# A fused convolution and quadratic-patch kernel in float32: matmul rounds regrouped by form, weight preparation spread over three engines, border taps on eight tiles

## What is computed

```python
y3 = conv(gn(x), w3, 'SAME') + b3          # 3x3, 32 -> 32 channels
y5 = conv(gn(x), w5, 'SAME') + b5          # 5x5, 32 -> 32 channels
stacked = [y5] + [y3 shifted by (ey, ex), zero padded, for the 9 shifts]
x = x + sum_g wr[c, g] * stacked[g] + br
spot = [1] + 3x3 patch of gn(x)            # 10 values a pixel and channel
x = x + einsum(spot[i] * spot[j], filters[o, c, i, j])
```

## Time and profile before

| | us |
|---|---|
| median of 3 runs (lowest, highest) | 365.67 (365.66, 366.77) |
| profiled execution | 365.12 |
| its span | 363.4 |
| first matmul starts | 30.07 |
| last matmul ends | 353.7 |
| PE busy | 323.6 |
| DVE, ACT, POOL busy | 188.3, 80.9, 5.2 |

### The profile page before, as it was taken

The page is one execution under the profiler, slowest core; times in us unless marked ns, Lnnn a source line. Parts: engine busy times, 40 slices in busy tenths (PEclk is TensorE's granted clock), DMA queues, the critical chain, the costliest instruction groups (busy, mean ns, idle before and its releaser), DMA issues.

```text
span 363.4 us, 15504 instructions
## 1 busy us (share of the span) xinstructions
PE 323.6 (89%) x7496; PEld 139.7 (38%) x7496; DVE 188.3 (52%) x227; ACT 80.9 (22%) x127; POOL 5.2 (1%) x28
## 2 busy tenths in 40 slices
PE   0006999999999999999999999999999999999990
PEld 0002544444544343344332247433334332247430
DVE  0399935504996035404499655429103679654036
ACT  1201025207337034500000003286000000000085
POOL 5000000000000000000000000000000000000000
PEclk9999999999999999999999999999999999999997
DMA  7943000000000000000000000055000000000046
GB/s 145 347 123 91 4 4 2 4 4 2 4 5 2 4 2 5 2 4 4 2 4 2 4 4 4 4 117 119 2 4 4 2 4 2 4 4 4 4 101 132
DMA packets 3297, 11.57 MB, mean 32 GB/s; under 512 B 804, under 2 KB 932, under 8 KB 3108
## 3 DMA queue, kind: packets, MB, share of 16 engines
q1 hardware_dynamic: 2656, 9.91, 10.1%
q10 hardware_dynamic: 484, 0.68, 0.8%
q0 software_dynamic: 96, 0.01, 0.5%
HBM read 6.40 MB, written 4.19 MB: 29 GB/s over the span
## 4 chain that ended last, share of the span: by engine, by line
PE 89%; DVE 5%; DMA 3%; ACT 1%; ACTq 1%; issue 0%; DVEq 0%
PE acc L570 87%; DMA w_in<-in_L_conv_w 3%; DVE raw L494 1%; PE acc L620 1%; DVE stats L449 1%; DVE folded L361 1%; PE acc L597 1%; ACT plane L265 0%; ACT folded L319 0%; ACTq L254 0%; ACTq L251 0%; DVE weight L362 0%; DVEq L81 0%; ACT w_taps L316 0%; PE acc L604 0%
## 5 line engine op out<-in xcount | busy, mean ns | idle before, releaser
L570 PE MATMUL acc<-product,weight 32*32 32x512 f32 (+1 forms) x4416 | 185.8, 601 | 0.0
L523 DVE TENSOR_TENSOR product<-plane 128x4096 f32<-128x4096 f32 x24 | 105.2, 4424 | 71.0 <-PE acc L570 70.9
L570 PE MATMUL acc<-plane,weight 32*64 32x512 f32 (+1 forms) x2048 | 102.0, 605 | 30.1 <-ACT plane L265 30.1
L570 PEld LDWEIGHTS acc<-product,weight 32*32 32x32 f32 (+1 forms) x4416 | 78.6, 111 | 106.8 <-issue 93.7
L570 PEld LDWEIGHTS acc<-plane,weight 32*64 32x64 f32 (+1 forms) x2048 | 39.5, 122 | 87.5 <-issue 84.7
L292 ACT ACTIVATE raw<-acc,offset_by_strip 32x512 f32<-32x512 f32 x44 | 29.8, 678 | 105.3 <-PE acc L570 104.6
L290 ACT ACTIVATE raw<-acc 32x512 f32<-32x512 f32 x48 | 28.2, 587 | 50.2 <-PE acc L570 49.5
L570 PE MATMUL acc<-plane,middle 32*64 32x512 f32 (+1 forms) x640 | 37.3, 593 | 0.0
L492 DVE COPY raw<-acc 32x512 f32<-32x512 f32 x16 | 11.1, 694 | 42.0 <-PE acc L570 41.7
L494 DVE TENSOR_SCALAR raw<-acc,offset_by_strip 32x512 f32<-32x512 f32 x20 | 15.1, 755 | 31.2 <-PE acc L570 30.8
L313 ACT ACTIVATE product<-plane 128x4096 f32<-128x4096 f32 x2 | 7.3, 3630 | 66.8 <-PE acc L570 66.7
(11 more groups left out here) (66 smaller groups left out, 45.1 us busy)
## 6 DMA issues: line engine op xcount, KB each, us to landing
raw<-in_x SPq DMA_DIRECT2D x8, 512.0 KB, 9.6
out<-raw SPq DMA_DIRECT2D x14, 256.0 KB, 3.0
filters_in<-in_L_conv_filters SPq DMA_DIRECT2D x4, 400.0 KB, 3.8
out<-raw ACTq DMA_DIRECT2D x2, 256.0 KB, 3.0
w_in<-in_L_conv_w SPq DMA_DIRECT2D x4, 100.0 KB, 3.3
w_in<-in_L_conv_w ACTq DMA_DIRECT2D x4, 36.0 KB
b_in<-in_L_conv_b POOLq DMA_DIRECT2D x2, 0.5 KB, 5.2
wr_in<-in_L_conv_wr ACTq DMA_DIRECT2D x1, 5.0 KB
```

Of the source, the lines that this page charges most:

```text
L523: nc.vector.tensor_tensor(product_rows(n), inner(g, 0, H), shifted(g, PRODUCTS[k]), ALU.mult)\
L570: return nc.tensor.matmul(acc[32 * s:32 * (s + strips), h, r, :], weights[32 * r:32 * r + 32, t:t + strips, :] .rearrange("p t c -> p (t c ...
```

## The change

- PE, stage 0: band 0 is now pairs of all five columns, borders, singles; band 1 is singles, borders, pairs, so that the next group's pairs follow in one round. `taps0`, `borders0` and `corners` replace the loop.
- PE, stage 1: `linear` and product 0 of both bands share three rounds; each later product does one form for both bands, and begins with the form the last one ended in. `PRODUCTS` is in another order for this, and the last two products are free only at `half_done`.
- Border columns: the right column goes to tiles (32r, 32(r+1 mod 4)), the left stays on (32r, 32r), and row taps and column taps alternate. ACT copies the right one with four instructions.
- Start: SP and ACT issue wr, w3 and w5 ahead of all images, ACT takes two of group 0's pieces, and SP takes the biases from POOL, behind group 0. DVE reorders w3 and goes on to the statistics. ACT scales the 3x3 taps once for each shift into `scaled3` (nine activations), POOL adds them to `folded` (nine adds, each waiting for the one before), and DVE transposes in two parts behind its part of the plane; PE waits for the first part for its first column.

```diff
-PRODUCTS = ((0, 0), (2, 2), (0, 1), (2, -2), (0, 2), (1, 2), (1, 1), (1, -2), (1, -1), (2, 1), (2, -1), (2, 0), (1, 0))
+PRODUCTS = ((0, 0), (0, 1), (2, 2), (2, -2), (1, 1), (1, -1), (2, 1), (1, 2), (0, 2), (2, -1), (1, -2), (1, 0), (2, 0))
...
-            if k == N_PRODUCTS - 1:
+            if k >= N_PRODUCTS - 2:
                 eng.wait_ge(half_done, N_HALVES + BANDS * (g + 1))
             else:
-                eng.wait_ge(product_used, (N_PRODUCTS - 1) * g + k + 1)
+                eng.wait_ge(product_used, (N_PRODUCTS - 2) * g + k + 1)
...
+        def load_small(eng, quarters):
+            if 0 in quarters:
+                eng.dma_start(wr_in[:, :], wr.rearrange("o g y x -> o (g y x)").partition_broadcast(GROUP))\
+                   .then_inc(small_in, 16)
+            else:
+                for r in range(GROUP):
+                    eng.dma_start(w5_in[32 * r:32 * r + 32, :], w5.rearrange("o c y x -> o (c y x)"))\
+                       .then_inc(taps5_in, 16)
+            for r in quarters:
+                eng.dma_start(w3_in[32 * r:32 * r + 32, :], w3.rearrange("o c y x -> o (c y x)")).then_inc(small_in, 16)
...
+            load_small(sp, (0, 1))
+            load_raw(sp, 0, (0, 2))
+            for n, v in enumerate((b3, b5, br)):
+                sp.dma_start(b_in[:, n:n + 1], v.rearrange("(o n) -> o n", n=1).partition_broadcast(GROUP))\
+                  .then_inc(bias_in, 16)
+            load_raw(sp, 1, range(PIECES))
...
+            pool.wait_ge(taps5_ready, 1)
+            five = folded[:, 0:TAPS0, :].rearrange("p (x y) c -> p x (y c)", x=5)
+            for n, (ey, ex) in enumerate(EY_EX):
+                pool.wait_ge(shift_scaled, n + 1)
+                three = scaled3[:, n, :, :].rearrange("p (x y) c -> p x (y c)", x=3)
+                part = five[:, ex + 1:ex + 4, C * (ey + 1):C * (ey + 4)]
+                nc.gpsimd.tensor_tensor(part, part, three, ALU.add).then_inc(shift_folded, 1)
+                if n < len(EY_EX) - 1:
+                    pool.wait_ge(shift_folded, n + 1)
...
+            load_small(act, (2, 3))
+            load_raw(act, 0, (1, 3))
...
+                nc.scalar.activation(columns[:, g, 0, :], acc[:, 1, 0, 0:H], ACT.Identity, bias=ring_bias[:, 14:15])
+                for r in range(GROUP):
+                    s = (r + 1) % STRIPS
+                    last = nc.scalar.activation(columns[32 * r:32 * r + 32, g, 1, :], acc[32 * s:32 * s + 32, 1, 1, 0:H],
+                                                ACT.Identity, bias=ring_bias[32 * s:32 * s + 32, 15:16])
...
-            nc.scalar.activation(w3_taps[:, :, :].rearrange("p (x y) c -> p x y c", x=3),
-                                 w3_in[:, :].rearrange("p (c y x) -> p x y c", y=3, x=3), ACT.Copy)
...
+            act.wait_ge(taps3_ready, 1)
+            for n, (ey, ex) in enumerate(EY_EX):
+                s = shift_index(ey, ex)
+                nc.scalar.activation(scaled3[:, n, :, :], w3_taps[:, :, :], ACT.Copy, scale=wr_in[:, s:s + 1])\
+                  .then_inc(shift_scaled, 1)
...
-            def fold_taps():
-                dve.wait_ge(taps_ready, 1)
...
-                    step(nc.vector.scalar_tensor_tensor(part, three, wr_in[:, s:s + 1], part, ALU.mult, ALU.add))
-                nc.vector.transpose(weight0[:, 0:TAPS0, :].rearrange("p t c -> p (t c)"),
-                                    folded[:, 0:TAPS0, :].rearrange("p t c -> p (t c)")).then_inc(weight0_ready, 1)
-                dve.wait_ge(weight0_ready, 1)
+            def reorder_taps():
+                dve.wait_ge(small_in, 80)
+                nc.vector.tensor_copy(w3_taps[:, :, :].rearrange("p (x y) c -> p x y c", x=3),
+                                      w3_in[:, :].rearrange("p (c y x) -> p x y c", y=3, x=3)).then_inc(taps3_ready, 1)
+            def turn_taps():
+                dve.wait_ge(shift_folded, len(EY_EX))
+                for a, b in ((0, 5), (5, TAPS0)):
+                    last = nc.vector.transpose(weight0[:, a:b, :].rearrange("p t c -> p (t c)"),
+                                               folded[:, a:b, :].rearrange("p t c -> p (t c)"))
+                    last.then_inc(weight0_ready, 1)
+                dve.wait_ge(weight0_ready, 2)
...
+                if phase == 0:
+                    turn_taps()
...
-            fold_taps()
+            reorder_taps()
...
-            def border_columns(g):
-                if g == 1:
+            def border_column_tap(g, t):
+                for side, col in enumerate((0, W - 1)):
+                    for r in range(GROUP):
+                        s = (r + side) % STRIPS
+                        at = PLANE_AT + t * PITCH + col
+                        last = nc.tensor.matmul(acc[32 * s:32 * s + 32, 1, side, 0:H],
+                                                weight0[32 * r:32 * r + 32, EDGE_AT + 5 * (2 + side) + t + 2, :],
+                                                plane[g][32 * r:32 * r + 32, at:at + (H - 1) * PITCH + 1:PITCH],
+                                                start=t == -2, stop=t == 2, tile_position=(32 * r, 32 * s))
+                return last
+            def borders0(g, h):
+                pe.wait_ge(edge_ready, 1)
+                if h == 0 and g > 0:
+                    wait_evicted(BANDS * g - 1)
+                for t in range(-2, 3):
+                    border_row_tap(g, h, t)
+                    if h == 0:
+                        last = border_column_tap(g, t)
+                if h == 0 and g == 1:
                     pe.wait_ge(weight1_ready, 1)
                     for s in range(STRIPS):
-                        nc.tensor.matmul(acc[32 * s:32 * s + 32, 1, 2, 0:2], weight1[0:32, CONST_AT, :],
-                                         ones[0:32, :], start=True, stop=True, tile_position=(0, 32 * s))
-                for t in range(-2, 3):
-                    for side, col in enumerate((0, W - 1)):
-                        for r in range(GROUP):
-                            at = PLANE_AT + t * PITCH + col
-                            last = nc.tensor.matmul(acc[32 * r:32 * r + 32, 1, side, 0:H],
-                                                    weight0[32 * r:32 * r + 32, EDGE_AT + 5 * (2 + side) + t + 2, :],
-                                                    plane[g][32 * r:32 * r + 32, at:at + (H - 1) * PITCH + 1:PITCH],
-                                                    start=t == -2, stop=t == 2, tile_position=(32 * r, 32 * r))
-                last.then_inc(columns_done, 1)
+                        last = nc.tensor.matmul(acc[32 * s:32 * s + 32, 1, 2, 0:2], weight1[0:32, CONST_AT, :],
+                                                ones[0:32, :], start=True, stop=True, tile_position=(0, 32 * s))
+                if h == 0:
+                    last.then_inc(columns_done, 1)
+                corners(g, h)
...
-            pe.wait_ge(weight0_ready, 1)
+            def taps0(g, h, pairs, start, stop):
+                for n, dx in enumerate(COLUMNS0):
+                    if g == 0 and h == 0 and pairs:
+                        pe.wait_ge(weight0_ready, min(n + 1, 2))
+                    if dx == 0:
+                        pe.wait_ge(middle_ready, g + 1)
+                    five = middle0[g] if dx == 0 else weight0[:, 5 * (dx + 2):5 * (dx + 3), :]
+                    last = column(h, plane[g], PLANE_AT, dx, range(-2, 3), five, start and n == 0,
+                                  stop and n == len(COLUMNS0) - 1, pairs)
+                return last
             for g in range(NG):
                 pe.wait_ge(plane_dve, g + 1)
                 pe.wait_ge(plane_act, g + 1)
-                for h in range(BANDS):
-                    if g > 0:
-                        wait_evicted(BANDS * (g - 1) + h)
-                    if h == 1:
-                        pe.wait_ge(columns_copied, g + 1)
-                    for pairs in (True, False):
-                        for n, dx in enumerate(COLUMNS0):
-                            if dx == 0:
-                                pe.wait_ge(middle_ready, g + 1)
-                            five = middle0[g] if dx == 0 else weight0[:, 5 * (dx + 2):5 * (dx + 3), :]
-                            if n == 2 and pairs:
-                                pe.wait_ge(edge_ready, 1)
-                                border_row(g, h)
-                                if h == 0:
-                                    if g > 0:
-                                        wait_evicted(BANDS * g - 1)
-                                    border_columns(g)
-                            last = column(h, plane[g], PLANE_AT, dx, range(-2, 3), five, n == 0,
-                                          n == len(COLUMNS0) - 1, pairs)
-                    last.then_inc(half_done, 1)
-            def taps1(g, h, k):
-                if k is None:
-                    for pairs in (True, False):
-                        for n, ix in enumerate((-1, 1, 0)):
```

(56 more changed lines are left out.)

72 lines of the change are left out of this document (30 added, 42 removed).

## The result

| | before | after |
|---|---|---|
| median (lowest, highest), us | 366.05 (365.66, 366.77) | 344.94 (344.8, 345.88) |
| ratio, 95% interval | | 0.9427 [0.9402, 0.9451] |
| span of the profiled execution | 363.4 | 343.1 |
| first matmul starts | 30.07 | 20.86 |

What follows compares the result with a forecast made beforehand. PE was taken to bound the kernel, busy 323.6 of 363.4 us. Start 19.5 + stream (323.66 - 9.3 - 2.4) + tail 9.7 = span 341.2; plus 1.7 and 0.55 gave 343.4, stated as 343.5; range 340.5 to 349, own range 340.5 to 345.

Steps and rivals of the forecast that it cites:

- Start 19.5: First matmul on PE expected at 19.5 instead of 30.07, a gain of 10.6 us; bounds 17 and 27.8.
- The plane's path: Before the first matmul: last image piece at 14.4, two statistics, then 3.9 us; ends at 19.5, last by a little.
- the weights' path: Before the first matmul: weights land at 8.0, ACT scales, POOL does nine adds, then a transpose; ends at 18.5.
- the rival: At the start: slow adds or late w3 make the weights set PE's start, 23 to 28; 347 to 352 us, chance 0.15.
- An add of 0.85: Each of POOL's nine adds at the start takes 0.85 us, DVE's 0.53 times 1.6.
- Rounds 9.3: PE's stream: fewer changes between pairs and singles, 84 rounds down to 25, save 9.3 us, range 8 to 10.
- Borders 2.4: Stage 0 border stretches: border columns on eight tiles instead of four save 2.4 us in all; 0.3 at the other end.
- The fullest-tile count (1.98): Border stretch on eight tiles: the fullest tile has a row's 0.70 and a column's 1.28, so 1.98 us instead of 3.26.
- column tiles that do not run together: Stage 0 borders: reading strided columns may be limited by the row group; 2.1 us comes back, 345.6 us, chance 0.22.
- PE's stream with no idle: Sign in the profile after: PE from first to last matmul takes 312 us and never idles.
- Stream 312.0: PE from first to last matmul: 323.66 less 9.3 for rounds and 2.4 for borders.
- waits none: Stages 0 and 1: no new PE wait replaces the savings; least margins 4 us at the last products, 1.08 at an eviction.

Runs made afterwards that it cites:

- one_add: The changed kernel with eight of POOL's nine adds replaced by a small memset, so its output differs; 343.51 us.
- warm_dve_add: The changed kernel with 64 extra 512-column matmuls on PE before its first real one, and the ninth add on DVE behind its plane write; 343.33 us.
- shift128: The changed kernel with 32 one-column matmuls (128 records) on PE ahead of the first real one; 343.35 us.
- cols_four: The changed kernel with the right border column back on the four tiles of the left one; 345.33 us.
- prewarm: The changed kernel with 64 extra 512-column matmuls on PE before its first real one, into banks written anew later; 343.67 us.
- shift64: The changed kernel with 16 one-column matmuls (64 records) on PE ahead of the first real one; 344.51 us.

## Why the prediction came out

The median was 344.94 for 343.5, in the range and in the forecast's own range. The saving came where it was forecast, but two steps were wrong, and the number is closer than they deserve, because smaller errors went the other way.

- **Start 19.5: measured 20.86.** The path was the wrong one. The plane's path alone gives 18.97 (one_add), 0.5 less than its sum; the weights' path set the start, by the mechanism of the rival but not at its price (23 to 28). Of the 18.5 summed for it, w3 landed at 9.13 and not 8.0 (+1.1), one scaling took 0.43 and not 0.7, an add 0.87 with its gap against 0.85. The rest is 1.1 us at the ninth add, held up by DVE's plane write: a contention that the sum had no term for. It touches the plane's path as well: by its rows that path would have started PE near 20.2 in the changed kernel (19.68, a transpose of 0.36, a signal of 0.14), 1.2 later than alone. That it was summed at 19.5 is in part luck: the last image was put at 14.4 and was in by 13.7, when DVE came to it.
- **An add of 0.85** held: 0.79 and a gap of 0.08. The Trainium skill's GPSIMD Engine Reference (Performance versus the Vector engine) gives 1.96 times VectorE. Here it was 1.5 times the 0.53 of DVE's fold of the same elements, from which the prediction worked, and 1.8 times the 0.45 that an add of this shape took on DVE itself (warm_dve_add); with DVE's long write beside it, more.
- **Rounds 9.3: about 9.6.** From shift128, which has no gap: its stream is 12.5 under the old, of which 2.75 are the borders and 0.1 a shorter slow beginning; 9.6 are left. cols_four gives 9.5 in the same way. Rounds of 320 pairs took 17.52 as predicted.
- **Borders 2.4: 2.75 in the stretches, some 1.0 in the end.** The fullest-tile count (1.98) was near: 1.81 and 2.05. The rival, column tiles that do not run together, fell: on eight tiles the stretch took 1.81 where it took 3.03 on four (cols_four). The rule of the Trainium skill (TensorE: Matmul & The Clock Gate, Part 3, The mechanism), that weight loads overlap running matmuls only when the row group differs, would have left it at 3.03, as the prediction applied it, and does not hold for these 64-element matmuls. But 0.87 + 0.86 came back as a stop of PE behind the borders, which "PE's stream with no idle" had excluded. This term of 1.7 us the sum put at nothing.
- **Stream 312.0: 312.6; waits none; tail 9.7: 9.6.** The stream is near because the stop of 1.7 met 0.3 more from the rounds, 0.35 more from the borders and a slow beginning shorter by 0.3. In stage 1 PE waited nowhere, and DVE still waits 63.9 us for PE.
- **Sum.** In the span the misses are 1.4 at the start and 0.6 in the stream, less 0.1 in the tail: 1.9. The median missed by 1.4 only, since the 0.55 us that the sum put between the profiled execution and the median came out at 0.06.

What stays open: why the slow beginning lasts between 2.9 and 6.0 us from kernel to kernel, and the first round so between 18.9 and 20.4, which no edit steered but prewarm.

## What to carry to other kernels

Where PE is busy all through, count the runs of one tile form, not the matmuls: each change of form cost some 0.17 us here, and grouping 84 into 25 was worth 9.6 us. When work moves from DVE to an idle POOL, put a term for each waiting out the other, above all for a long DVE write in which the last POOL instruction of the path begins. When a dense stretch of tiny matmuls gains less than counted, look for PE "issue" behind it, and shift the program by some records before you rewrite the stretch.

## What the hardware showed that was not expected

- Behind 272 records of matmuls and weight loads in 1.8 us PE stood 0.55 us without waiting for anything shown, and the gap depended on the place in pieces of 256 records (0.55 and 0.20 at no shift, 0.60 and 0.41 at 256, none and 0.10 at 64, none at 128).
- The slow beginning of PE is not in the clock column, which reads 1.00 throughout. The pace shows it; shift64, its first round in two windows:

```profile
20.87:26.80 5.93, 5.93 (x56) 1.00 0.44 103
26.80:41.27 14.47, 14.47 (x272) 1.00 0.30 75
```

106 ns a record, then 53: half pace, as between the levels of 1.2 and 2.4 GHz, for 5.9 us, where the changed kernel had it for 3.4. The trace's own record of the granted clock bears this out: it begins, at full rate, where the pace doubles (26.82 in shift64, 24.32 in the changed kernel, 34.03 before, 12.94 in prewarm), and the column's 1.00 ahead of that stands for no record at all. Work that ends 3.26 us earlier takes the slow beginning away (prewarm).
- DVE and POOL waited for each other's whole instructions. A one-element DVE instruction that reads two tensors took 0.65 us for 0.16 (L491), since it ended only with POOL's add; a 2560-column write that met an add lost 0.44; and an add that began within that write ended 0.65 us behind it and took 1.92 for 0.79.
